# Two expert layers of a vision tower: products over 96 + 96 rows become products over 128 and 64 rows, the 64-row ones on the two halves of TensorE's array

## The reference, cut to what matters

```python
# layer "L0_ffn": 8 experts, D=192, H=512, two choices per token, W1 is (8, 192, 1024)
xg = xpad[buf]                                     # up to 120 rows per expert and choice
h = jnp.einsum('ecd,edh->ech', xg, W1)
act = h[..., :H] * jax.nn.silu(h[..., H:])
ye = jnp.einsum('ech,ehd->ecd', act, W2)
# layer "L2_ffn": 16 experts, D=192, 768 hidden, 100 rows per expert
gate = jax.nn.silu(jnp.einsum('ecd,efd->ecf', xg, Wg))
up = jnp.einsum('ecd,efd->ecf', xg, Wu)
out = jnp.einsum('ecf,edf->ecd', gate * up, Wd) * topk_score[..., None]
```

## Time and profile before

| | |
|---|---|
| median of 3 runs | 1153.18 us |
| profiled execution, its own time | 1157.56 us |
| its span (first to last instruction) | 1155.8 us |
| PE busy / PEld busy | 895.9 us (78%) / 761.3 us (66%) |
| DVE / ACT / POOL busy | 528.1 / 332.2 / 261.5 us |
| mean granted TensorE clock over the span | 0.835 of full |
| stage 2's products (L2389), first to last start | 330.7 to 407.1 us |
| stage 6's products (L2624), first to last start | 849.9 to 977.2 us |

### The profile page before, as it was taken

The page is one execution under the profiler, slowest core; times in us unless marked ns, Lnnn a source line. Parts: engine busy times, 40 slices in busy tenths (PEclk is TensorE's granted clock), DMA queues, the critical chain, the costliest instruction groups (busy, mean ns, idle before and its releaser), DMA issues. The chain is left out here.

```text
span 1155.8 us, 31081 instructions
## 1 busy us (share of the span) xinstructions
PE 895.9 (78%) x13412; PEld 761.3 (66%) x13412; DVE 528.1 (46%) x1168; ACT 332.2 (29%) x677; POOL 261.5 (23%) x289
## 2 busy tenths in 40 slices
PE   8889986998359926898856695777779999387594
PEld 5678863886359915788755573656479998265472
DVE  1469954544353146554522365562920111464464
ACT  0257732212112212442442133343101122133132
POOL 1168841330134214211200101111033322200100
PEclk9989997777569977898876698885969999598698
DMA  9047857300358220000004200001438981100000
GB/s 261 11 120 183 179 151 244 80 1 1 119 169 208 54 65 1 2 3 1 2 1 115 71 4 1 2 3 38 113 89 215 253 217 15 30 3 1 2 4 23
DMA packets 58450, 88.29 MB, mean 76 GB/s; under 512 B 10756, under 2 KB 45000, under 8 KB 58340
## 3 DMA queue, kind: packets, MB, share of 16 engines
q1 hardware_dynamic: 53220, 81.85, 26.6%
q0 software_dynamic: 5120, 4.88, 2.3%
HBM read 78.30 MB, written 7.30 MB: 74 GB/s over the span
## 5 line engine op out<-in xcount | busy, mean ns | idle before, releaser
L2660 DVE TENSOR_TENSOR L_ffnhid<-L_ffnact_gate,L_ffnbank_u 128x300 f32<-128x300 f32 x32 | 14.9, 467 | 118.9 <-ACT L_ffnact_gate L2679 110.2
L1717 PE MATMUL ps_places<-stage_own_y,stage_spread 80*64 80x128 f32 x800 | 55.7, 288 | 2.1 <-issue 2.1
L1807 POOL TENSOR_SCALAR stage_hat_x<-stage_hat_x 128x320 f32<-128x320 f32 x40 | 51.2, 1279 | 19.7 <-ACT stage_hat_x L1783 19.7
L1867 DVE TENSOR_TENSOR stage_product<-ps_rows,stage_hat_x 128x960 f32<-128x960 f32 x40 | 46.3, 1158 | 17.7 <-PE ps_rows L1728 16.0
L1728 PE MATMUL ps_rows<-stage_strip,stage_hat_y 64*32 64x96 f32 x3200 | 49.7, 254 | 2.5 <-issue 1.7
L1717 PEld LDWEIGHTS ps_places<-stage_own_y,stage_spread 80*64 80x64 f32 x800 | 45.5, 142 | 8.3 <-issue 2.8
L1728 PEld LDWEIGHTS ps_rows<-stage_strip,stage_hat_y 64*32 64x32 f32 x3200 | 40.5, 108 | 10.1 <-issue 10.1
L2593 POOL DMA_INDIRECT stage_y_rows<-L_ffndown,stage_choice_index x16 | 25.4, 1589 | 90.5 <-ACT L_ffndown L2686 57.3
L1872 DVE TENSOR_REDUCE stage_samples<-stage_product 128x120 f32<-128x960 f32 x40 | 45.7, 1145 | 0.0
L1110 PE MATMUL L_attnbank_q<-L_attnhT,L_attnwq 128*128 128x200 f32 x192 | 41.5, 361 | 5.2 <-DVE L_attnqT L1275 5.0
L1815 POOL TENSOR_TENSOR stage_hat_x<-stage_rel_x,stage_w_column 128x160 f32<-128x160 f32 x80 | 35.1, 461 | 45.6 <-POOLq L1522 45.6
(11 more groups left out here) (427 smaller groups left out, 2262.3 us busy)
## 6 DMA issues: line engine op xcount, KB each, us to landing
stage_strip<-in_strips SPq DMA_DIRECT2D x80, 189.0 KB
L_ffn_win<-in_L_ffn_Win SPq DMA_DIRECT2D x10, 1152.0 KB
stage_L_ffn_win<-in_L_ffn_Win SPq DMA_DIRECT2D x6, 1152.0 KB
L_ffnranks<-stage_ranks SPq DMA_DIRECT2D x16, 400.0 KB
L_ffn_win<-in_L_ffn_Win SPq DMA_DIRECT2D x8, 768.0 KB
L_ffn_wout<-in_L_ffn_Wout SPq DMA_DIRECT2D x10, 576.0 KB
stage_L_ffn_wout<-in_L_ffn_Wout SPq DMA_DIRECT2D x6, 576.0 KB
L_ffn_wout<-in_L_ffn_W SPq DMA_DIRECT2D x8, 384.0 KB
```

Source lines behind the costliest of these rows:

```text
L1717: mm = nc.tensor.matmul(ps_places[HALF_P * h:HALF_P * (h + 1), p % 2, g * P:(g + 1) * P], k.spread[:, p * GRID + g, :], places[:, h * P:(h ...
L1807: nc.gpsimd.tensor_scalar(x, x, 1.0, 1.0, ALU.min, ALU.subtract).then_inc(s["hat_x"], 1)
L1867: nc.vector.tensor_tensor(products(i % 2), in_psum(i % 2), weights_x(i % BUFFERS), ALU.mult).then_inc(s["multiplied"], 1)
```

## The change

`win` becomes one array of 128 partitions. Inputs 0 to 127 of the gate product lie in its first third, inputs 64 to 191 of the up product in its second; its last third holds on partitions 0 to 63 the up product's inputs 0 to 63, and on partitions 64 to 127 the gate product's inputs 128 to 191. The transposes make two overlapping pieces of 128 inputs (0 to 127 and 64 to 191). Each `up(e, c)` now has a group of whole products (128 rows, gate then up, tile by tile) and a group of rest products (64 rows: up on array rows 0 to 63, gate on rows 64 to 127, alternating). For c=0 the rest group goes first, for c=1 the whole group. The number of products is the same, 8 per `up` in stage 2 and 12 in stage 6. The bytes of `win` are the same.

```diff
@@ experts_by_pair (experts_by_row: the same with C for 2 * C) @@
-        xT = sb("xT", [HALF, 2, HALVES, 2 * C])
+        xT = sb("xT", [P, 2, 2, 2 * C])
...
-                for h in range(HALVES):
-                    for k in range(2):
-                        mm = nc.tensor.transpose(ps_x[:, e % 2, h, k * C:(k + 1) * C], x[0:C, e, k, h * HALF:(h + 1) * HALF], tw.identity[0:C, 0:C])
+                for k in range(2):
+                    own = slice(k * C, (k + 1) * C)
+                    nc.tensor.transpose(ps_x[:, e % 2, 0, own], x[0:C, e, k, 0:P], tw.identity[0:C, 0:C])
+                    mm = nc.tensor.transpose(ps_x[:, e % 2, 1, own], x[0:C, e, k, REST:DIM], tw.identity[0:C, 0:C])
...
-                for f in range(fb):
-                    for ps, at in ((ps_g, 0), (ps_u, hidden)):
-                        o = at + (c * fb + f) * P
-                        for k in range(HALVES):
-                            mm = nc.tensor.matmul(ps[:, c, f, :], weights.win[e % NB][:, k, o:o + P], xT[:, e % 2, k, :], start=(k == 0), stop=(k == 1))
+                mm = weights.project_in(nc.tensor, e, c, fb, xT[:, e % 2], ps_g[:, c], ps_u[:, c])
@@ ExpertWeights @@
-            self.win.append(tw.sb(f"{self.name}_win{b}", [HALF, HALVES, 2 * self.hidden]))
+            self.win.append(tw.sb(f"{self.name}_win{b}", [P, 3 * self.hidden]))
...
-        sp.dma_start(self.win[b][:], self.w_in[e].rearrange("(k q) n -> q k n", q=HALF)).then_inc(self.loaded[b], 16)
+        sp.dma_start(self.win[b][:], self.w_in[e]).then_inc(self.loaded[b], 16)
...
+    def project_in(self, pe, e, c, count, xT, gate, up):
+        w = self.win[e % len(self.win)]
+        low, high = slice(0, REST), slice(REST, P)
+        tiles = [(f, slice((c * count + f) * P, (c * count + f + 1) * P)) for f in range(count)]
+
+        def whole(first):
+            for f, at in tiles:
+                flags = {"start": first and f == 0, "stop": not first and f == count - 1}
+                pe.matmul(gate[:, f, :], w[:, at], xT[:, 0, :], **flags)
+                mm = pe.matmul(up[:, f, :], w[:, self.hidden + at.start:self.hidden + at.stop], xT[:, 1, :], **flags)
+            return mm
+
+        def rest(first):
+            for f, at in tiles:
+                flags = {"start": first and f == 0, "stop": not first and f == count - 1}
+                own = slice(2 * self.hidden + at.start, 2 * self.hidden + at.stop)
+                pe.matmul(up[:, f, :], w[low, own], xT[low, 0, :], **flags)
+                mm = pe.matmul(gate[:, f, :], w[high, own], xT[high, 1, :], **flags)
+            return mm
+
+        for i, part in enumerate((rest, whole) if c == 0 else (whole, rest)):
+            mm = part(i == 0)
+        return mm
@@ layout @@
+    def gate_and_up(gate, up):
+        rest = np.concatenate([up[:, :REST], gate[:, P:]], 1)
+        return np.concatenate([gate[:, :P], up[:, REST:], rest], 2)
```

More of the change, by code:

```diff
@@ L24 @@
 HALF = DIM // HALVES
+REST = DIM - P
 GROUPS = HEADS // 4
@@ L2311, in experts_by_pair @@
         bank_x, bank_g, bank_u, bank_d = pb("bank_x"), pb("bank_g"), pb("bank_u"), pb("bank_d")
-        ps_x = bank_x[0:HALF, :, 0:HALVES * 2 * C].rearrange("q b (k c) -> q b k c", k=HALVES)
+        ps_x = bank_x[:, :, 0:2 * 2 * C].rearrange("q b (k c) -> q b k c", k=2)
         ps_g, ps_u = (b[:, :, 0:fb * 2 * C].rearrange("p b (f c) -> p b f c", f=fb) for b in (bank_g, bank_u))
@@ L2557, in experts_by_row @@
         x = sb("x", [C, n_exp, DIM])
-        xT = sb("xT", [HALF, 2, HALVES, C])
+        xT = sb("xT", [P, 2, 2, C])
         act_gate = sb("act_gate", [P, 2, fb, C])
@@ L2562, in experts_by_row @@
         bank_x, bank_g, bank_u, bank_d = pb("bank_x"), pb("bank_g"), pb("bank_u"), pb("bank_d")
-        ps_x = bank_x[0:HALF, :, 0:HALVES * C].rearrange("q b (k c) -> q b k c", k=HALVES)
+        ps_x = bank_x[:, :, 0:2 * C].rearrange("q b (k c) -> q b k c", k=2)
         ps_g, ps_u = (b[:, :, 0:fb * C].rearrange("p b (f c) -> p b f c", f=fb) for b in (bank_g, bank_u))
@@ L2611, in turn @@
                     pe.wait_ge(s["xT_ready"], e - 1)
-                for k in range(HALVES):
-                    mm = nc.tensor.transpose(ps_x[:, e % 2, k, :], x[:, e, k * HALF:(k + 1) * HALF], tw.identity[0:C, 0:C])
+                nc.tensor.transpose(ps_x[:, e % 2, 0, :], x[:, e, 0:P], tw.identity[0:C, 0:C])
+                mm = nc.tensor.transpose(ps_x[:, e % 2, 1, :], x[:, e, REST:DIM], tw.identity[0:C, 0:C])
                 mm.then_inc(s["x_in_psum"], 1)
@@ L3153, in layout @@
     o["L0_ffn_Wg"] = a["L0_ffn_Wg"]
-    o["L0_ffn_Win"] = np.concatenate([a["L0_ffn_W1"][..., h:], a["L0_ffn_W1"][..., :h]], 2)
+    def gate_and_up(gate, up):
+        rest = np.concatenate([up[:, :REST], gate[:, P:]], 1)
+        return np.concatenate([gate[:, :P], up[:, REST:], rest], 2)
+    o["L0_ffn_Win"] = gate_and_up(a["L0_ffn_W1"][..., h:], a["L0_ffn_W1"][..., :h])
     o["L0_ffn_W2"] = a["L0_ffn_W2"]
     o["L2_ffn_gate"] = a["L2_ffn_gate_weight"].T
-    o["L2_ffn_Win"] = np.concatenate([a["L2_ffn_Wg"].transpose(0, 2, 1), a["L2_ffn_Wu"].transpose(0, 2, 1)], 2)
+    o["L2_ffn_Win"] = gate_and_up(a["L2_ffn_Wg"].transpose(0, 2, 1), a["L2_ffn_Wu"].transpose(0, 2, 1))
     o["L2_ffn_Wout"] = a["L2_ffn_Wd"].transpose(0, 2, 1)
```

## The result

The changed kernel took 1120.95 us (median of 4 runs, 1116.72 to 1123.05) where the kernel before, on the same chip, took 1153.01: ratio 0.9743, 95% interval 0.9695 to 0.9791. The same changed kernel, run again later, gave 1125.11 (6 runs, 1120.83 to 1135.03), ratio 0.9798 (0.9733 to 0.9862).

The account below looks back on a forecast made before the run. TensorE was taken to bound stages 2 and 6; savings of 8.5 and 15.1 us, 23.6 together, took the 1153.2 us median to 1129.6, forecast as 1130 us, range 1122 to 1153.

Parts of the forecast that it names:

- TensorE sets the pace of both stages: Stages 2 and 6 run at TensorE's pace from first rows to last product; an expert's saved time is the program's.
- Pair slots of 203 and 112 ns: Two 64-row products side by side cost 203 ns in stage 2, 112 in stage 6, saving 1.62 and 1.34 us an expert.
- Rivals 1 and 3: Rival 1: half-height weight loads queue, 1152 us, chance 0.13. Rival 3: 64-row products do not overlap, 1163 us, chance 0.12.
- Switches of 0.20 and 0.18 us: Changing between 128-row and 64-row products costs 0.20 us in stage 2, 0.18 in stage 6, twice an expert.
- Wider transposes: Transposes of 128 instead of 96 columns cost at most 0.1 us an expert in stage 2, 0.03 to 0.06 in stage 6.
- The sum: Stage 2 saves 8.5 us and stage 6 15.1, together 23.6 us off the profiled 1157.56.
- The cold part: Stage 6's first three halves, before the clock rises: 2.6 us saved, half lost again to the clock, leaving 1.3.
- Rival 2: Stage 6: POOL's scatter chain stalls ACT and TensorE, or the clock rises later; 6 to 8.5 us lost, about 1137, chance 0.15.
- the two bounds of the text: DMA rate of the `win` loads to 128 partitions: the same as before, or 1.6 times; taken as hidden.
- all other stages keep their time: The sum counted savings in stages 2 and 6 only, with no term for any other stage.

Follow-up runs that it names:

- the kernel without overlap: Changed kernel with both rest products of a tile on the lower 64 array rows; 1158.83 us, ratio to the kernel before 1.0076.
- the pair with six products: Six unused products ahead of each even tile's wait in stage 3, added to both kernels: kernel before 1153.87 us, changed kernel 1118.83 us.

## Why the prediction was right, point by point

**TensorE sets the pace of both stages: right.** In the changed stage 6 it waits for nothing over 1 us between the first product and the last output.

**Pair slots of 203 and 112 ns: right**, by the timelines and by the kernel without overlap. L1728's row was the right neighbour. The Trainium skill's "TensorE: Matmul & The Clock Gate", LDWEIGHTS, read strictly (two loads of 112 ns, one behind the other), would have made a pair cost 0.22 us in stage 6; the pair of 64 x 128 loads takes 0.11, so "TensorEngine Tiling (Array Packing)", Key Properties, is the rule that the trace bears out. Rivals 1 and 3 fall with it.

**Switches of 0.20 and 0.18 us: right**, found by fitting L242 and L243 with the columns and confirmed by four more of them. They show as two gaps of 0.10 on either side of the first record, not as the one gap I described.

**Wider transposes: +0.1 us an expert in stage 2 did not come.** Hence periods of 8.28 and 6.49 where the text gave 8.4 and 6.5.

**The sum: near in total in the profiled pair, and partly by luck.** Stage 2: turn to turn 1.22 us less, not 1.12, and the first two experts gained 1.65 and 1.47; 11.8 us against the 8.5 forecast, 0.7 of it earlier gathered rows. Stage 6: from the third turn to the last output product 14.6 us less (13.8 forecast for the warm experts). The cold part gained 4.1 us, 0.97 and 3.08 in the first two turns, not 1.3: I had the clock rise after as much time as before, and it rose 14.5 us behind the first product instead of 20.4. The stage started 1.4 us later and its end lost 3.9 us, below. That leaves 13.3 against 15.1. Together 25.1 against 23.6. In stage 2 too the clock rose sooner, 4.4 us behind the first product and not 7.0. But this pair is the one with the smallest gain. Five profiles with the changed stage 6 (nothing added in it) took 178.8 to 186.7 us there, 182.1 in the mean, and five with the old one 198.7 to 200.5, mean 199.8: 17.7 us. With the 11.3 us of stage 2, taken the same way over four and four, the change is worth some 29 us in its own stages.

**Rival 2 came in part, at the end of the stage.** The scatters of the changed kernel, POOL's timeline, answering:

```profile
936.83 1.56 POOL L2615 DMA_INDIRECT stage_y_rows<-L_ffndown,stage_choice_index  x1 [3.70 <-ACT L_ffndown L2704]
941.39 1.57 POOL L2615 DMA_INDIRECT stage_y_rows<-L_ffndown,stage_choice_index  x1 [2.99 <-DMA stage_y_rows<-L_ffndown,stage_choice_index]
946.11 1.56 POOL L2615 DMA_INDIRECT stage_y_rows<-L_ffndown,stage_choice_index  x1 [3.15 <-DMA stage_y_rows<-L_ffndown,stage_choice_index]
```

The last output product started at 938.86; the chain of scatters was behind and reached its last one only at 946.11. From that output product to the barrier it takes 18.3 us, against 14.4 before and with stage 6 changed alone, where the last scatter waited for ACT. While weights were loading ACT waited 5.2 us in all for scatters, and one period was 6.65. Not every execution pays for the end: in the later profile it took some 2 us less, and with stage 6 alone nothing more than before. Where the weights load, the DMAs are close to full:

```profile
870.42:876.92 6.50, 6.50 (x65) 6.28 (x63) 0.94 (x2) 1.48 (x4) 2.63 (x2) 1.00 0.95 311
```

311 GB/s at a share of 0.95, against 260 at 1.07 before: 1.2 times the rate, between the two bounds of the text, 1.0 and 1.6. Most of that is the shorter period, since the same weights pass in 6.5 instead of 7.5 us. By the DMA engines' busy time, 311/0.95 against 260/1.07, the new layout moves 1.35 times the bytes, and so it does in the kernel without overlap (243 GB/s at 0.73).

**The steps that failed** are two. One the sum did not have: that all other stages keep their time. Stage 3 gave 10.4 us in the profiled pair. It was in the rows to be had: a stage with 2.4 us waits whose clock had fallen at each of three. In five of the fourteen profiles it took 179.5 to 181.2 us (two of them with three products in the waits), in seven, none of them filled, 189.9 to 192.1; the other two are those with six products. Two profiles of the changed kernel have one each, so it is no gain of the change: in the profiled pair it was luck. What decides when the clock rises in stage 3, and so which of the two an execution gets, stays open.

The other is a term that was too small: stage 6's first experts, put at 1.3 us because the clock was to rise after as much time as before. It rose 20.4 to 20.5 us behind the first product in three of the five profiles with the old stage 6 and 17.2 and 18.0 in the others, but 14.5 in three and 6.7 to 6.8 in two of the five with the changed one. The first two turns gained 4.1 us in the first profile of the changed kernel and 7.7 in the later one. Why it rose sooner isn't shown.

It would be wrong to lay the 9 us between the forecast and the first median to stage 3 alone. With stage 3 the same in both, in the pair with six products, the change is still worth 35.0 us by the medians (4 and 10 runs) and 31.3 between the two profiled executions, and the two stages changed one at a time give 29.8. What part stage 3 has in the executions that weren't profiled isn't known.

## What to carry to other kernels

When a contraction isn't a multiple of 128 rows, cut it into full products and 64-row halves that run side by side: here a pair cost as much as one product, weight loads included, and a switch 0.2 us, so group them. A saving at TensorE's pace is read per period and multiplied; what cannot be read off so is the granted clock, in the stage's own first microseconds and in stages that weren't touched, so split a difference by stage before it is explained, and compare executions with like clocks. A few idle-time products that compute nothing can be worth more than they cost (10 us here), if they fit into the wait; count records, not products.

## What the runs showed of the hardware that was not expected

- Two 64 x 128 weight loads, in the upper and lower half of the array, start together and pass at 0.11 us a pair, the price of one 96 x 128 load.
- At the same 2.4 us idle time of TensorE the clock fell in two executions (34.51 and 34.54 us behind its last rise) and held in three (34.60, 34.61, 34.90), and then did the same at the next two waits. Where the wait ended 27.0 to 27.6 us behind a second rise, it fell in all five. Products in the wait kept it up in all four kernels that had them.
- In stage 6 the clock stayed at 1.2 GHz for 14.5 us behind the first product in three profiles of the changed stage, although TensorE was busy all that time (14.45 of 14.45 us), and for 6.7 to 6.8 us in two. In both kernels with five products of 512 columns ahead it was at 2.4 GHz from the first product on.
- Weights loaded to 128 partitions with runs a third longer moved 1.35 times the bytes per busy time of the DMA engines (311 GB/s at a share of 0.95, against 260 at 1.07). Which of the two does it isn't shown.
